# A fused convolution and window-attention kernel: the filling in front of TensorE's placed code is executed instead of jumped over

## The reference

```python
x = x + conv3x3(_gn(x), weight)              # 256 -> 256 channels, padding 1
qkv = einsum('nchw,oc->nohw', windows4x4(_gn(x)), qkv_w)
msq = concat([qkv, avg_pool5(qkv)])          # inside each window
q, k, v = relu(..), relu(..), ..             # 64 heads of 8 channels
kv = einsum('ngld,nglm->ngdm', k, v_and_ones)
out = einsum('ngld,ngdm->nglm', q, kv); out = out[..., :-1] / out[..., -1:]
x = x + batch_norm(einsum('nchw,oc->nohw', out, proj_w))
```

## The kernel before

| site | instructions since the site before | reached at slot | filling |
|---|---|---|---|
| LEAD, images 1 to 6 | 2183 from slot 56 | 191 | 217, over a block's end |
| LEAD, image 0 | what the runtime puts ahead isn't known | - | unknown |
| LOOP, images 0 to 6 | 666 from slot 152 | 50 | 42 |
| OUT0, all images | 928 from slot 92 | 252 | 84, over a block's end |
| OUT1, all images | 461 from slot 80 | 29 | 27 |
| FIRST, image 7 | 2204 from slot 56 | 212 | 124, over a block's end |
| LOOP, image 7 | 429 from slot 80 | 253 | 95, over a block's end |

## Time and profile before

### The profile page before, as it was taken

The page is one execution under the profiler, slowest core; times in us unless marked ns, Lnnn a source line. Parts: engine busy times, 40 slices in busy tenths (PEclk is TensorE's granted clock), DMA queues, the critical chain, the costliest instruction groups (busy, mean ns, idle before and its releaser), DMA issues.

```text
span 2417.3 us, 112385 instructions
## 1 busy us (share of the span) xinstructions
PE 2366.7 (98%) x49576; PEld 2150.9 (89%) x49576; DVE 1730.8 (72%) x3206; ACT 1451.0 (60%) x3754; POOL 1170.9 (48%) x2365
## 2 busy tenths in 40 slices
PE   7999999999999999999999999999999999998998
PEld 7998899888998889988899888998889988897887
DVE  9887658767587765877658766687766876665764
ACT  2158861588516884178832788327882288813886
POOL 0037750477405773057730677216771167712776
PEclk9999999999999999999999999999999999999999
DMA  4000010000200001000010000100001000000000
GB/s 171 1 2 16 19 65 10 2 19 16 75 1 6 15 20 71 1 6 19 16 71 1 7 18 16 71 1 9 16 20 66 1 9 19 21 9 2 16 16 25
DMA packets 39114, 58.37 MB, mean 24 GB/s; under 512 B 4704, under 2 KB 36064, under 8 KB 36832
## 3 DMA queue, kind: packets, MB, share of 16 engines
q1 hardware_dynamic: 38880, 55.27, 6.4%
HBM read 29.57 MB, written 25.69 MB: 23 GB/s over the span
## 4 chain that ended last, share of the span: by engine, by line
PE 95%; DVE 2%; issue 1%; DMA 0%; ACT 0%; SPq 0%; POOL 0%; POOLq 0%; DVEq 0%
PE ps L354 33%; PE ps L425 15%; PE ps L373 12%; PE ps L414 10%; PE ps L400 9%; PE ps L380 9%; PE ps L389 4%; PE ps L434 3%; DVE dp L883 1%; DMA xs<-w_conv 0%; PE ps L336 0%; DVE xs L896 0%; DVE kv_part L989 0%; PE ps L365 0%; DVE rcp L999 0%
## 5 line engine op out<-in xcount | busy, mean ns | idle before, releaser
L354 PE MATMUL ps<-dp,wc 128*128 128x392 f32 x4608 | 840.8, 341 | 0.2 <-DVE dp L883 0.2
L354 PEld LDWEIGHTS ps<-dp,wc 128*128 128x128 f32 x4608 | 815.3, 188 | 5.3 <-issue 3.1
L1204 POOL TENSOR_TENSOR ve<-vpraw,vmask 128x1024 f32<-128x1024 f32 x200 | 381.0, 1905 | 349.8 <-ACT vpraw L665 349.8
L425 PEld LDWEIGHTS ps<-at,wp 128*128 128x128 f32 x3200 | 373.1, 191 | 47.5 <-DVE kvm L1016 46.4
L425 PE MATMUL ps<-at,wp 128*128 128x128 f32 (+1 forms) x3200 | 404.7, 280 | 1.0 <-ACT yb L700 1.0
L1175 POOL TENSOR_TENSOR qm<-qraw 128x64 f32<-128x64 f32 x200 | 59.5, 298 | 700.5 <-ACT qraw L672 699.9
L636 ACT CAST dp<-dt 128x896 fp32r<-128x896 f32 x128 | 121.0, 945 | 449.0 <-PE ps L354 356.3
L373 PE MATMUL ps<-wkv,xt 128*128 128x512 f32 x1200 | 324.8, 406 | 1.6 <-issue 1.6
L654 ACT ACTIVATE ve<-ps,vmask 128x256 f32<-128x256 f32 x800 | 314.3, 491 | 0.0
L414 PEld LDWEIGHTS ps<-kvm,qs 64*32 64x32 f32 x25088 | 233.5, 105 | 90.8 <-issue 88.8
L1016 DVE TENSOR_TENSOR kvm<-ps,hm 128x576 f32<-128x576 f32 (+1 forms) x400 | 277.4, 734 | 2.9 <-PE ps L400 2.8
(11 more groups left out here) (86 smaller groups left out, 3110.3 us busy)
## 6 DMA issues: line engine op xcount, KB each, us to landing
out<-xs SPq DMA_DIRECT2D x224, 112.0 KB, 1.8
xs<-x SPq DMA_DIRECT2D x14, 1344.0 KB, 7.5
xs<-x SPq DMA_DIRECT2D x14, 224.0 KB, 2.7
xs<-w_conv SPq DMA_DIRECT2D x2, 1152.0 KB, 12.2
xs<-x SPq DMA_DIRECT2D x2, 896.0 KB, 6.6
xs<-x SPq DMA_DIRECT2D x2, 672.0 KB, 7.8
kvm<-w_kv SPq DMA_DIRECT2D x1, 512.0 KB, 13.7
wp<-w_proj SPq DMA_DIRECT2D x4, 128.0 KB, 9.9
```

Source lines behind the costliest of these rows:

```text
L354: last = nc.tensor.matmul(ps[:, conv_bank(v, mt), 0:CONV_N], wc[:, part_w, k, kt * TAPS + dy, mt * P:(mt + 1) * P], dp[:, kk % 2, part_d, ...
L425: last = nc.tensor.matmul(ps[:, BANK_A + mt, Y0:Y0 + n], wp[:, q, mt * P:(mt + 1) * P], at[:, q, e, 0:n], start=(q == 0), stop=(q == QUADS ...
L1204: nc.gpsimd.tensor_tensor(ve[:, t % 2, :, 1].rearrange("p e (n m) -> p e n m", m=DIM + 1)[:, :, :, 0:DIM], vpraw[:].rearrange("p (n m) -> ...
```

## The change

The fillers are the same in number and place, and what follows them stands at the same slots. What was passed by one branch is now executed from the first filler to the last.

```diff
             def at_slot(offset):
-                pe.addr_align(bass.FETCH_BLOCK_INSTRUCTIONS, offset=offset, max_nops=0)
+                pe.addr_align(bass.FETCH_BLOCK_INSTRUCTIONS, offset=offset, max_nops=bass.FETCH_BLOCK_INSTRUCTIONS - 1)
```

## The result

The kernel after takes 2577.45 us (median of 6 runs, 2572.92 to 2580.92), the kernel before 2419.26 in the same comparison (6 runs). The ratio is 1.0654, 95% interval 1.0640 to 1.0668: 158 us slower. The prediction was 2538 us, in a range from 2440 to 2606. The profiled execution took 2576.49 us, 157.4 more than the profiled one of before (2419.14).

A forecast was written before the change was run, and what follows sets the result against it. TensorE's stream was taken as the bound (PE busy 2366.7 of 2417.3 us). Images 1 to 6 88.2, image 0 5.6, image 7 13.4 and clock 11.6 made 118.8 us on 2419.14: 2538 us, range 2440 to 2606.

The forecast's parts named there:

- sequencer time less cover: At each filled site, fillers times 65 ns less 0.35 us for the branch, less the work PE already had queued.
- 162: Upper-end loss in us over the whole kernel, with each filler taking 87 ns.
- the 187: Loss in us at 87 ns per filler with a clock fall after each OUT0 as well, giving 2606 us.
- Price of one filler: Sequencer time for each executed filler: 65 ns taken, between 57 (the gap alone) and 87 (like a MOVE).
- LEAD: Images 1 to 6: 217 fillers delay issue by 13.75 us; less 3.04 of queued work, PE idles 10.7 us each.
- The clock: After PE's idle stretch at six LEADs and at FIRST of image 7, 1.65 us each, 11.6 us in all.
- at OUT0 I count none: No clock loss after about 3.5 us idle at OUT0; kept for the upper end of the range.
- LOOP and OUT0: LOOP, images 0 to 6: 0.7 us lost each, the fetch wait hiding the rest; OUT0, all images: 3.3 us each.
- OUT1: All images: issue 1.4 us later, covered by matmuls already queued, so nothing lost; the stall at 99 matmuls stays.
- Cheap fillers: Rival: fillers take 12 to 57 ns, mostly LEAD loses; 2441 us at 25 ns, 2456 at 30; chance 20%.
- fillers passed like matmuls: Rival: about 6 ns per filler, hidden at every site, no change, 2419 to 2421 us; chance 13%.
- The rival of a gain: Block fetches start earlier without branches, removing L414's 16.5 us of stalls: 2403 us, or 2411 for half; chance 4%.

## Why the prediction was right

**Direction and size.** It went by the right mechanism, sequencer time less cover, and came out 39 us low: 119 us forecast, 158 measured. Both missing parts are terms of its sum, so the result inside the range isn't luck. One figure of the working is off: with 87 ns it gives 164 us idle and 176 with the clock, where "162" leaves the clock out; the 187 at the end of the range has it.

**Price of one filler.** 65 ns was taken between 57 and 87; it is 74. The gap between two sequencer instructions was read rightly, and a filler does 13 ns of its own. Putting 74 into the same working gives 12.67 at each LEAD, 0.8 at LEAD of image 0 with its 57, 1.1 at LOOP, 4.1 at OUT0, 6.8 and 5.2 in image 7: 129 us, against 127.4 of idle time measured and 107 forecast. That is 22 us of the miss.

**The clock.** 11.6 us was the term that was mis-sized; PE's busy time grew by 31.4. The step that failed is "at OUT0 I count none", and that LOOP was not thought of at all. The forecast counted seven falls of 1.65 us, half of the 3.3 us at a granted clock of 0.50 in the earlier trace rows. No run shows 1.65 us as the cost of a fall. The trace has 22: they cost about 2 us each at the six LEADs (12.4 us in the run with LEAD alone) and about 1.2 us each at the other sixteen. So the number was wrong far more than the size. The mean granted clock is 0.969, so an estimated (1 - 0.969) x 2574.7 / 0.5 = 160 us were spent at half clock. Part of that costs nothing, since PE idles in it: 7.2 of 10.2 us at LEAD of image 1, 1.25 of 6.8 at OUT0 and next to nothing at LOOP. The forecast took one row, a fall after 2.37 us idle, and yet counted none for the 3.5 us that it expected at OUT0.

**LEAD.** Idle 12.5 against 10.7, at the place named, six times. The rule count x 0.074 - 3.39 gives 12.7 for it, 4.6 with 108 fillers (4.46 measured) and nothing with 39 (none measured in image 1). Nothing behind it won any of it back: the run with LEAD alone lost the 90 us that its idle time and clock make.

**LOOP and OUT0.** Idle 2.2 and 4.4, for a loss of 1.1 and about 4 after taking off the stalls that were there before; 0.7 and 3.3 were forecast. At LOOP the fetch did hide part of the fillers, as said.

**OUT1.** "Nothing lost" was right for the issue and wrong for the fetch. Alone it costs about 1 us each, by the late start of the next block's fetch; the sum had no term for that.

**The rivals.** Cheap fillers, or fillers passed like matmuls, are refuted by the 2760 rows of the fillers. The rival of a gain, that running through lets the fetch start when the block is entered, was tested without the fillers' price and is the wrong way round: behind a branch the fetch came after about 1.0 us, and without branch or filler it came later, 1.5 us behind the wait in image 3. At these sites the branch's target is in the same block or the next, and the fetch was earliest behind a branch. What stays open is what starts the fetch where there is no branch.

## What to carry to other kernels

An executed filler cost TensorE's sequencer 74 ns here, so by this estimate the branch (0.35 us) is cheaper from five of them on, and the 217 of LEAD, 16.0 us, were covered only for the 3.04 us of work that PE had queued. On an engine as busy as PE here (98%), count a starved microsecond as idle time and then something for the clock behind it, also after stretches as short as the 2.2 us at LOOP: here 31.4 us of longer busy time came with 127.4 us of idle time. Where short matmuls run into the end of a block of instructions, look for "issue" stalls at a constant count of matmuls, like the 79, 87 and 99 of the earlier trace rows. Placing the code moved them here (to 100 with LOOP at slot 50), and a taken branch 3.4 us ahead of the block's end and in front of a wait brought that of image 1 from 1.02 down to 0.19 us.

## What was not expected of the hardware

- A filler is 13 ns long in the trace and takes 74 ns of the sequencer.
- The clock fell after 2.2 us without a matmul, at six of seven LOOPs in one run and at three of seven in another, and behind stalls of 1.5 to 1.8 us in the run with LOOP at slot 50.
- Behind a taken branch the fetch of the following block came sooner (1.0 us to the packet, against 1.75 behind the first of 27 fillers). Moving the branches of LOOP and OUT1 13 instructions ahead gained 0.3%.
- Ten rounds over a body of 925 instructions fetched nothing again, placed or not (144 and 133 fetches in all; in the kernel before q8 has no packet between 480 and 612 us, in the loop of image 1).
- Where the code stands is worth 1.7% in this kernel, at an unchanged stream of work.
